# Graph network on one Trainium2 core: the bias product of the norm stages on full 4-byte words

## The reference, cut to what matters

```
def _gcn_conv(x, W, b, src, dst, dinv):
    h = x @ W
    norm = dinv[src] * dinv[dst]
    agg = segment_sum(h[src] * norm[:, None], dst)
    agg = agg + (dinv * dinv)[:, None] * h
    return agg + b

x = _gcn_conv(node_embedding, W1, b1); x = _l2norm(x)
def f(z):
    z1 = _l2norm(_gcn_conv(z, Wf1, bf1))
    return _gcn_conv(z1, Wf2, bf2) + z
k1 = f(x); k2 = f(x + 0.5 * k1); k3 = f(x + 0.5 * k2); k4 = f(x + k3)
x = x + (k1 + 2.0 * k2 + 2.0 * k3 + k4) / 6.0
return _gcn_conv(x, W2, b2)
```

## Time and profile before

| What | Value |
|---|---|
| median of 3 runs | 6430.47 us (6430.21 to 6433.66) |
| the profiled execution | 6431.79 us, span 6429.9 us |
| mean granted TensorE clock | 0.809 |
| busy: PE / DVE / POOL / ACT | 80% / 73% / 61% / 44% |
| norm stage 0, first to last product of sums | 2086.7 to 2444.0 us |
| norm stage 1 | 2802.6 to 3160.8 us |
| norm stage 2 | 3519.7 to 3877.5 us |
| norm stage 3 | 4237.8 to 4683.5 us |
| norm stage 4 | 4996.7 to 5290.8 us |

### The profile page before, as it was taken

One profiled execution on the slowest core, in us unless ns is written; L12 is line 12 of the kernel. 1 busy time (PEld: TensorE's weight loads), 2 busy tenths in 40 slices (PEclk: granted clock), 3 DMA queues, 4 the chain that ended last, 5 costly groups with the idle time before them and its releaser, 6 DMA issues. The chain is left out here.

```text
span 6429.9 us, 101948 instructions
## 1 busy us (share of the span) xinstructions
PE 5150.1 (80%) x25772; PEld 4128.5 (64%) x25772; DVE 4720.9 (73%) x14274; ACT 2819.0 (44%) x8831; POOL 3923.0 (61%) x3976
## 2 busy tenths in 40 slices
PE   7499999995777778987799778976679558967776
PEld 3389999994766446854487446853368447755654
DVE  8467777775665456867687776878878788888886
ACT  7167777773444553322233222322223236644442
POOL 1277777777554665557655765555556776566664
PEclk9699999997999557965599558965589559989897
DMA  0289988874554667988898888989989555534342
GB/s 2 43 218 261 262 254 258 263 234 129 158 163 156 209 216 258 323 264 287 263 324 283 285 288 280 323 294 341 341 268 282 165 163 162 160 124 122 122 124 79
DMA packets 930902, 1406.59 MB, mean 219 GB/s; under 512 B 157981, under 2 KB 453981, under 8 KB 930355
## 3 DMA queue, kind: packets, MB, share of 16 engines
q1 hardware_dynamic: 664979, 898.20, 43.7%
q0 software_dynamic: 138368, 296.57, 17.1%
q10 hardware_dynamic: 127008, 205.58, 8.7%
HBM read 852.92 MB, written 547.19 MB: 218 GB/s over the span
## 5 line engine op out<-in xcount | busy, mean ns | idle before, releaser
L1390 DVE SCALAR_TENSOR_TENSOR c_rows<-bank,carry,c_rows 32x256 f32<-32x256 f32 (+2 forms) x1950 | 888.6, 456 | 899.2 <-PE bank L1754 506.0
L1754 PE MATMUL bank<-c_rows,sums_all 128*128 128x256 f32 (+1 forms) x1960 | 1112.4, 671 | 532.7 <-DVE c_rows L1390 516.1
L1398 POOL DMA_INDIRECT c_rows<-y_tab,src_pair x784 | 757.0, 966 | 602.2 <-PE bank L1754 382.4
L1754 PEld LDWEIGHTS bank<-c_rows,sums_all 128*128 128x128 f32 x1960 | 489.8, 310 | 965.9 <-DVE c_rows L1390 948.3
L1398 POOL DMA_INDIRECT c_rows<-t_tab,src_pair x784 | 741.1, 945 | 519.8 <-PE bank L1982 360.6
L1773 ACT ACTIVATE c_squares<-c_y,c_root 128x256 f32<-128x256 f32 x784 | 391.7, 500 | 1022.8 <-DVE c_y L1859 779.9
L1752 PE MATMUL bank<-bias_rows,c_degs 128*128 128x256 f32 (+1 forms) x980 | 695.6, 710 | 26.7 <-DMA c_degs<-kap_tab 26.7
L2025 ACT ACTIVATE c_xt<-bank 128x512 f32<-128x512 f32 x392 | 234.1, 597 | 906.2 <-PE bank L1991 906.2
L760 PE MATMUL bank<-w_mix,lxt 128*128 128x256 f32 x2400 | 607.3, 381 | 1.9 <-ACT lxt L1029 1.9
L760 PE MATMUL bank<-w_mix,c_xt 128*128 128x256 f32 x2352 | 605.9, 380 | 0.0
L761 PE MATMUL bank<-bias_rows,two_r 128*128 128x256 f32 (+1 forms) x1400 | 595.2, 427 | 0.0
(11 more groups left out here) (388 smaller groups left out, 13010.8 us busy)
## 6 DMA issues: line engine op xcount, KB each, us to landing
c_z<-t_tab SPq DMA_DIRECT2D x490, 256.0 KB
y_tab<-ly SPq DMA_DIRECT2D x400, 256.0 KB
t_tab<-lt SPq DMA_DIRECT2D x400, 256.0 KB
c_own<-y_tab SPq DMA_DIRECT2D x392, 256.0 KB
t_tab<-c_y ACTq DMA_DIRECT2D x392, 256.0 KB
c_own<-t_tab SPq DMA_DIRECT2D x392, 256.0 KB
c_z<-y_tab SPq DMA_DIRECT2D x294, 256.0 KB
y_tab<-c_y ACTq DMA_DIRECT2D x294, 256.0 KB
```

The costliest lines, as they stand in the source:

```text
L1390: nc.vector.scalar_tensor_tensor(rows, before[p0:p0 + 32, :], m["carry"][p0:p0 + 32, t:t + 1], rows, ALU.mult, ALU.add).then_inc(S["carrie ...
L1398: pool.indirect_dma_start(out=two(m["c_rows"], j % 4, H2)[:, i, 0:w], out_offset=None, in_=source, in_offset=bass.IndirectOffsetOnAxis(ap= ...
L1754: nc.tensor.matmul(out, sums[:, 2 * j + i, :], two(rows, j % 4, H2)[:, i, 0:w], start=False, stop=True).then_inc(S["summed"], 1)
```

## The change

One line in the norm stages. The two operands of the bias product are read as plain F32 instead of F32R; the bytes in memory are the same. The product is then issued as two matmul instructions with two weight loads, like every other plain F32 product. The instructions stand in the same order as before on all engines, and every wait stays.

```diff
@@ norm_stage, add_up
-                nc.tensor.matmul(out, degs[:, j % 8, i * P:(i + 1) * P], bias_of(m, bias), start=True, stop=False)
+                nc.tensor.matmul(out, degs[:, j % 8, i * P:(i + 1) * P].bitcast(F32), bias_of(m, bias).bitcast(F32), start=True,
+                                 stop=False)
                 pe.wait_ge(S["carried"], st.at("carried", 2 * j + i + 1))
                 nc.tensor.matmul(out, sums[:, 2 * j + i, :], two(rows, j % 4, H2)[:, i, 0:w], start=False, stop=True
                                  ).then_inc(S["summed"], 1)
```

## The result

The changed kernel takes 6224.84 us in the median of 4 runs (6216.18 to 6232.21), the kernel before 6431.36 (6430.21 to 6433.66): a ratio of 0.9678, interval 0.9661 to 0.9695.

A forecast was written before the change was run, and what follows sets the result against it. The prediction took the PE-DVE chain at the low clock to bound norm stages 0 to 2, transfers stage 3, POOL stage 4. Savings of 60 + 92 = 152 us gave 6431.8 - 152 = 6280, range 6232 to 6345.

The forecast's parts named there:

- The step that failed: Norm stage 3: transfers fill its 4.55 us a pair, so at most 5 us could be gained; 0 was taken.
- its low end: Whole kernel: 60 + 122 + 5 = 187 us less, 6245, and a little beyond if POOL's cycle is shorter.
- the sign: Norm stage 3: a pair clearly under 4.5 us would show that the transfers were not full there.
- The sizes of stages 0 to 2: Norm stage 0: 60 us less at 3.01 a pair; stages 1 and 2: 46 less each at 3.17.
- The chain at the higher clock: PE and DVE in norm stages at clock 1.00: sums 0.60 us, a step 1.16, a pair 2.3; not the next bound.
- the 50 for stage 0 in the high end of the range: Norm stage 0's share of the smallest forecast gain, 50 + 48 - 10 = 88 us less, 6344.
- The clock: Norm stages 0 to 2: rises from 0.50 to 1.00 within the first few pairs and stays up despite PE gaps.
- rival A: Clock stays at 0.50, only work is added: up to 41 us in stages 0 to 2, about 10 in stage 4; chance 0.06.
- Rival B: Clock rises and falls in turn, half of the stages' pairs fast: 76 us less, 6355; chance 0.06.
- Rival C: Transfers give the clock's gain back, norm stages 1 and 2 keep 3.55 a pair: 80 us less, 6352; chance 0.06.
- the condition: Norm stages 0 to 2: the clock rises because PE's gap closes, streaming 1.72 us of a 1.83 us step instead of 1.10.

The follow-up runs named there:

- A table less: One of three table transfers left out in norm stage 3: on the kernel before 6434.87 us, on the changed kernel 6224.64 us.
- a shorter DVE instruction: Kernel before, with the third term in norm stage 3 added on 32 of 512 columns only, all transfers kept: 6386.4 us, ratio 0.9929.
- The double inversion: POOL's inversion made twice in all norm stages: on the changed kernel 6409.64 us, on the kernel before 6480.91 us.
- The rounded product four times: Kernel before, bias product kept on rounded words (F32R) but issued four times into the same bank: 6219.83 us, ratio 0.9675.
- the version that holds the clock: Changed kernel, with the full-word (plain F32) bias product made twice in norm stage 3 and on rounded words in stage 4: 6213.15 us, ratio 0.966.
- Twice the rounded product: Kernel before, bias product kept on rounded words (F32R) but issued twice: 6267.21 us, ratio 0.9743.

## Why the prediction was wrong, point by point

**The step that failed** is this term of the sum: **"norm stage 3: it is full of transfers, 4.55 x 0.99 leaves 0.05 x 98 = 5 at the most; I take 0".** The stage gave 38 us, of the 55 by which the norm stages together gave more than forecast; with them the forecast would have been 6242 and its low end near 6200, and the measured time would have lain inside. The DMA share was read as a ceiling. A table less left the stage at its time, and a shorter DVE instruction made it faster with all transfers in place. The prediction named the sign itself: a pair clearly under 4.5 us would mean that the transfers were not full. What should have been read is DVE's order in stage 3 of the kernel before:

```profile
4501.76 0.49 DVE L1390 SCALAR_TENSOR_TENSOR c_rows<-bank,carry,c_rows 32x256 f32<-32x256 f32 x1 [0.53 <-PE bank L1754]
4502.29 0.69 DVE L1871 SCALAR_TENSOR_TENSOR c_rest<-c_z,c_rest 128x512 f32<-128x512 f32 x1
...
4503.08 0.88 DVE L1859 SCALAR_TENSOR_TENSOR c_y<-c_y,c_inv,c_rest 128x256 f32<-128x256 f32 x2
4503.88 0.68 DVE L1866 TENSOR_TENSOR c_rest<-c_z 128x512 f32<-128x512 f32 x1
4504.60 0.47 DVE L1390 SCALAR_TENSOR_TENSOR c_rows<-bank,carry,c_rows 32x256 f32<-32x256 f32 x1
4505.00 0.85 DVE L1832 SCALAR_TENSOR_TENSOR c_y<-bank,lead,c_own 128x256 f32<-128x256 f32 x2
4506.38 0.49 DVE L1390 SCALAR_TENSOR_TENSOR c_rows<-bank,carry,c_rows 32x256 f32<-32x256 f32 x1 [0.53 <-PE bank L1754]
```

A pair of 4.62 us, in which DVE never waits but for the sums, once, 0.53. The same order after the change, begun at the other carry:

```profile
4301.76 0.47 DVE L1390 SCALAR_TENSOR_TENSOR c_rows<-bank,carry,c_rows 32x256 f32<-32x256 f32 x1
4302.16 0.85 DVE L1833 SCALAR_TENSOR_TENSOR c_y<-bank,lead,c_own 128x256 f32<-128x256 f32 x2
4303.04 0.49 DVE L1390 SCALAR_TENSOR_TENSOR c_rows<-bank,carry,c_rows 32x256 f32<-32x256 f32 x1
4303.57 0.69 DVE L1872 SCALAR_TENSOR_TENSOR c_rest<-c_z,c_rest 128x512 f32<-128x512 f32 x1
4304.36 0.88 DVE L1860 SCALAR_TENSOR_TENSOR c_y<-c_y,c_inv,c_rest 128x256 f32<-128x256 f32 x2
4305.16 0.68 DVE L1867 TENSOR_TENSOR c_rest<-c_z 128x512 f32<-128x512 f32 x1
4305.88 0.47 DVE L1390 SCALAR_TENSOR_TENSOR c_rows<-bank,carry,c_rows 32x256 f32<-32x256 f32 x1
```

4.12 us, and no wait. Where the clock is low for a moment the 0.53 is back, which is what holding the clock saved. Over the whole stage DVE's carries waited for the sums as follows (us, times; before, after, and with the clock held):

```profile
  DVE c_rows L1390: 69.2, 104
...
  DVE c_rows L1390: 28.9, 32
...
  DVE c_rows L1390: 15.5, 6
```

These are 40 and 13 us less, where the stage took 38 and 11.7 less. About 10 us of each are one wait at the start. In the kernel before, none of PE, DVE, ACT and POOL waited for a transfer in this stage, but for PE once, at its start.

**The sizes of stages 0 to 2** were 5 to 7 us low each. Stage 0 came to 2.97 a pair where 3.01 was read off stage 4 and four pairs were left at the low clock; the clock was up after two tiles. For stages 1 and 2 I had put the floor at the transfers, 3.17; they came to 3.12. The double inversion shows that POOL sets the pace there too. Its gathers got longer, in stage 1 from a mean of 963 ns before (as in stage 0) to 1038 here; why is not shown. More traffic alone is not it: with the inversion twice they take 1044 at 281 GB/s, before the change 963 at 278. This is their line in stage 1 of the changed kernel (the number behind the first comma is the mean, the last group is the idle time by what ended it):

```profile
L1398 POOL DMA_INDIRECT c_rows<-y_tab,src_pair x188 | 195.1, 1038 | 52.1 <-issue 49.2 <-PE bank L1755 2.9
```

Waits of POOL for PE, 65 to 87 us in a stage before, are 2.9 here, as the prediction said of stage 0, where they are 9.9. The chain at the higher clock was mis-sized too: the sums take 0.70 us and a step 1.31 to 1.33, not 0.60 and 1.16. That cost nothing, since two steps still lie under POOL's 3 us. And the 50 for stage 0 in the high end of the range is worked out nowhere.

**What was right.** The clock: 1.00 within the first tiles of stages 0 to 2, and a mean of 0.97 to 0.99 over the whole of them, with DVE's wait for the sums gone as the bound. The rounded product four times shows that this is PE's work and not the words. That the clock would stay up with waits in every step came true in these stages and not in stage 3 (0.79); nothing in the prediction told them apart, and no run shows why they differ, only that the product on full words twice holds it at 1.00 in stage 3 too. No delay from the added product: rival A's price never came due. Rival B, the swing, was right for stage 3 alone, where the clock is 0.79, and costs little there (11.7 us by the version that holds the clock), since DVE sets the pace. Rival C did not come: stages 1 and 2 run at 324 GB/s. Stage 4 stayed where POOL holds it, at clock 0.50.

**Half right: the condition.** I expected the rise because PE's gap closes. Twice the rounded product leaves a gap and raises the clock too. The rise came as forecast, but a reader who took the closed gap as a rule would have missed nearly four fifths of the gain at two fifths of the work.

## What to carry to other kernels

Where a serial chain crosses TensorE and its profile shows the low clock, work that fills TensorE's waits can pay for itself: look at the granted clock of each stage before counting instructions, and then read the next bound of every stage one by one, from the order of its busiest in-order engine. A DMA share near 1 with no engine waiting for a transfer was no bound here. To learn whether an engine is the bound of a stage, add to its work in both kernels: it costs in the one and not in the other.

## What the runs showed of the hardware that was not expected

- The DMA share can stand above 1: 1.03 and 1.04 in stage 3, at 371 to 383 GB/s, where the same stage showed 0.99 at 341.
- Stages with nearly the same busy share of PE sit at either clock: norm stage 0 before at 78% and 0.50, after at 79% (227.91 of 290 us) and 0.97. Nor does the length of PE's waits tell the level: with the rounded product twice the clock stayed at 1.00 from 2100 to 2127 us with waits of 0.37 to 0.43 in all steps but one (0.72), and fell after one of 1.60; waits of 0.37 to 0.43 left it at 0.50 throughout stage 0 before. What decides is not shown.
